# Retention and feed-forward kernel, one core: states summed into other banks, and the order of the batch loop turned

## The reference

```python
xn = layernorm(x)                              # per token over 128 features
q, k, v = xn @ Wq, xn @ Wk, xn @ Wv            # 8 heads of 16
# retention in chunks of 64 tokens, per head:
attn    = (q_c @ k_c.T) * D                    # decayed causal mask
o_intra = attn @ v_c
o_inter = (q_c * decay_q) @ S
S       = decay_s * S + (k_c * decay_k).T @ v_c
att = concat_heads(o_intra + o_inter) @ Wo
h = xn @ w1 + gate * low_rank(xn)              # w1, w2 are ternary with a scale for each row
ffn = (relu(h) ** 2) @ w2
out = x + att + ffn
```

## Time and profile before

| what | value |
|---|---|
| runs | 129.81, 127.7, 129.81 us; median 129.81 |
| the profiled execution | 129.01 us, of which the span of the instructions is 127.0 us |
| PE busy | 117.0 us (92%) |
| DVE busy | 99.2 us (78%) |
| ACT busy | 78.7 us (62%) |
| POOL busy | 64.0 us (50%) |
| TensorE granted clock, mean | 0.997 |
| chain that ended last | PE 80%, DVE 10%, issue 4%, ACT 2%, POOL 1% |

### The profile page before, as it was taken

How to read it: one execution, slowest core, us unless ns; L and a number is a source line. 1 busy time by engine, 2 the same in 40 slices (tenths; PEclk the granted TensorE clock), 3 DMA queues, 4 the chain that set the end, 5 groups by cost and what they waited for, 6 DMA issues and landing times.

```text
span 127.0 us, 6564 instructions
## 1 busy us (share of the span) xinstructions
PE 117.0 (92%) x2860; PEld 92.8 (73%) x2860; DVE 99.2 (78%) x261; ACT 78.7 (62%) x158; POOL 64.0 (50%) x60
## 2 busy tenths in 40 slices
PE   4979999988999999499999999999999999499991
PEld 4425869856688778377788778878897889377890
DVE  0788795489799969858699979896999799729832
ACT  3265669967871897227972897188738774382910
POOL 7099803984439161923439252916193529544400
PEclk9999999999999999999999999999999999999998
DMA  3849920000023000400023001300020002000202
GB/s 105 296 149 320 389 92 34 0 3 5 8 90 81 5 0 23 145 7 0 0 92 74 0 0 53 112 0 0 0 83 0 0 0 83 0 5 0 88 5 83
DMA packets 3357, 7.71 MB, mean 61 GB/s; under 512 B 384, under 2 KB 896, under 8 KB 3216
## 3 DMA queue, kind: packets, MB, share of 16 engines
q1 hardware_dynamic: 2880, 7.01, 16.3%
q10 hardware_dynamic: 464, 0.50, 1.2%
HBM read 5.42 MB, written 2.10 MB: 59 GB/s over the span
## 4 chain that ended last, share of the span: by engine, by line
PE 80%; DVE 10%; issue 4%; ACT 2%; POOL 1%; DVEq 0%; POOLq 0%
PE ps_work L659 10%; PE ps_score L735 8%; PE ps_work L663 7%; PE ps_work L660 7%; PE ps_score L705 6%; PE ps_score L747 5%; PE ps_score L781 5%; PE ps_y L761 4%; PE ps_y L762 4%; PE ps_score L720 3%; DVE sums_of L532 3%; PE ps_turn L668 3%; PE ps_y L765 2%; DVE xn L491 2%; PE ps_turn L692 1%
## 5 line engine op out<-in xcount | busy, mean ns | idle before, releaser
L300 POOL TENSOR_TENSOR sq_lo<-square,sq_hi 128x512 fp32r<-128x512 f32 x31 | 39.8, 1295 | 36.2 <-ACT sq_hi L356 36.2
L347 ACT ACTIVATE square<-ps_work 128x512 f32<-128x512 f32 x32 | 19.1, 596 | 23.1 <-PE ps_work L663 22.6
L516 DVE TENSOR_TENSOR scores<-ps_score,cst 128x512 f32<-128x512 f32 x32 | 20.3, 682 | 1.6 <-PE ps_score L705 1.6
L305 POOL TENSOR_TENSOR q_pair<-q_dec,cst 128x1024 f32<-128x1024 f32 x7 | 13.3, 1894 | 15.9 <-DVE q_dec L501 15.9
L356 ACT ACTIVATE sq_hi<-square 128x512 fp32r<-128x512 f32 x32 | 20.1, 627 | 0.1
L352 ACT ACTIVATE square<-square 128x512 f32<-128x512 f32 x32 | 18.9, 630 | 0.1
L491 DVE TENSOR_SCALAR xn<-x_in,mean_var,rstd 128x128 f32<-128x128 f32 x32 | 14.9, 528 | 0.3
L659 PE MATMUL ps_work<-xn_hi,w_hi 128*128 128x512 f32 x32 | 14.3, 447 | 0.4 <-issue 0.4
L735 PE MATMUL ps_score<-scores,v_pad 64*32 64x64 f32 x1024 | 12.5, 225 | 1.6 <-issue 1.6
L663 PE MATMUL ps_work<-xn_lo,w_hi 128*128 128x512 f32 x32 | 12.6, 394 | 0.0
L660 PE MATMUL ps_work<-xn_hi,w_lo 128*128 128x512 f32 x32 | 12.6, 393 | 0.0
(11 more groups left out here) (123 smaller groups left out, 238.6 us busy)
## 6 DMA issues: line engine op xcount, KB each, us to landing
x_in<-x_tok SPq DMA_DIRECT2D x8, 256.0 KB, 3.4
resid<-x_feat SPq DMA_DIRECT2D x1, 2048.0 KB, 7.7
out_feat<-resid SPq DMA_DIRECT2D x7, 256.0 KB
po_in<-ffn_weights SPq DMA_DIRECT2D x1, 320.0 KB, 3.2
fc_in<-ffn_weights SPq DMA_DIRECT2D x1, 256.0 KB, 3.7
q_table<-q_decay SPq DMA_DIRECT2D x1, 256.0 KB, 3.5
wqvk<-qvk_weights ACTq DMA_DIRECT2D x1, 192.0 KB, 3.9
cst<-const ACTq DMA_DIRECT2D x1, 129.0 KB, 3.9
```

Of the source, the lines that this page charges most:

```text
L300: nc.gpsimd.tensor_tensor(sq_lo[p][:, f, :], square[p][:, f, :], sq_hi[p][:, f, :].bitcast(F32), ALU.subtract).then_inc(lo_ready, 1)
L347: nc.scalar.activation(square[b.parity][:, f, :], ps_work[f % 2][:], ACT.Relu).then_inc(relu_ready, 1)
L516: nc.vector.tensor_tensor(scores[:, g].rearrange("p t s i -> p (t s) i"), ps_score[:, g].rearrange("p (a i) -> p a i", i=BLK), causal.unsq ...
```

## The change

Banks: `ps_turn` and `ps_y` become the two halves of one tensor `ps_both`. Both sides of v and k by token go there in every batch, the first too, and `gather_states` sums into it, no longer into banks 2 and 3 of `ps_score`. The masks run in the order 0 to 3. The first layer's weight is built in bank 3 of `ps_score` and not in `ps_y`.

Order: `gather_states` follows `score` directly. `own_values` and `carry` of batch b stand in front of q, k, v of b+1, in the same body, where `carry` stood in the next one. The turning of `xn` of b+1 waits for all states of b to be read. On VectorE the statistics are taken two batches ahead, `variance` stands behind `decay_q`, `take_states` between the first and the second mask, `add_states` behind `low_xn`, `low_o` of b at the end of b's own body. On ScalarE `root` and `high_o` move with them. On GpSimd `spread_q` stands behind all four `low_square`. In VectorE's and ScalarE's lists the last two of the six bodies are written out (`over_middle`). Products of one column (`place_program`) stand at three places; the warm-up's wide products are fewer.

```diff
+        ps_both = pb("ps_both", [P, ROWS, SEQ])
+        ps_turn, ps_y = ps_both[:, 0, :], ps_both[:, 1, :]
+        w1_bank = ps_score[:, NG - 1, :]
 GpSimd:
             def body(b):
-                for f in range(2):
+                for f in range(NF):
                     low_square(b, f)
                 spread_q(b.step(1))
-                for f in range(2, NF):
-                    low_square(b, f)
 ScalarE:
+            def body(b, more):
                 take_relu(b, 0)
                 take_relu(b, 1)
-                root(b.step(1))
+                take_relu(b, 2)
                 take_square(b, 0)
+                high_square(b, 0)
                 take_square(b, 1)
-                high_square(b, 0)
-                high_o(b.step(-1))
-                take_relu(b, 2)
+                take_relu(b, 3)
+                round_xn(b.step(1))
                 high_square(b, 1)
-                round_xn(b.step(1))
-                take_relu(b, 3)
                 take_square(b, 2)
+                high_square(b, 2)
                 take_square(b, 3)
-                high_square(b, 2)
+                high_square(b, 3)
+                high_o(b)
                 copy_k(b.step(1))
                 copy_k_tok(b.step(1), 0)
-                high_square(b, 3)
                 copy_k_tok(b.step(1), 1)
+                if more:
+                    root(b.step(2))
 VectorE:
+            def body(b, more):
+                before, after, later = b.step(-1), b.step(1), b.step(2)
-                statistics(after)
-                statistics_done(after)
-                take_states(before)
-                variance(after)
-                for k in range(3):
-                    add_states(before, k)
                 for step in range(4):
                     inverse_root(after, step)
                 normalise(after)
-                low_o(before)
+                mask_scores(b, 0)
+                take_states(b)
+                for g in range(1, NG):
+                    mask_scores(b, g)
                 low_xn(after)
-                for g in MASK_ORDER[:2]:
-                    mask_scores(b, g)
+                for k in range(3):
+                    add_states(b, k)
                 finish(before, ps_y)
+                if more:
+                    statistics(later)
+                    statistics_done(later)
                 decay_q(after)
-                for g in MASK_ORDER[2:]:
-                    mask_scores(b, g)
+                if more:
+                    variance(later)
+                low_o(b)
-                for side in range(2):
-                    take_v(after, side)
+                take_v(after, 0)
+                take_v(after, 1)
 TensorE:
             def gather_states(b):
                 pe.wait_ge(zeroed, ZEROED)
-                pe.wait_ge(scores_ready, b.count(NG, ROWS))
+                pe.wait_ge(v_ready, b.count(2, 2))
...
-                            ins = mm(ps_score[g * GW:(g + 1) * GW, ROWS + r, t * GW:(t + 1) * GW],
+                            ins = mm(ps_both[g * GW:(g + 1) * GW, r, t * GW:(t + 1) * GW],
+            def place_program(n, bank, data):
+                for k in range(n):
+                    rows = slice(k % NG * GW, (k % NG + 1) * GW)
+                    mm(bank[rows, 0:1], data[rows, 0:GW], data[rows, 0:1], start=True, stop=True, skip_group_check=True)
...
+            own_values(first)
+            place_program(17, ps_score[:, NG - 1, :], ident)
+            carry(first)
+            def hidden_and_scores(b):
                 pe.wait_ge(q_ready, b.count(1, 1))
                 hidden(b, 0)
                 pe.wait_ge(k_ready, b.count(1, 1))
                 hidden(b, 1)
+                hidden(b, 2)
+                pe.wait_ge(o_lo_ready, b.count(1, 0))
+                score(b)
+                gather_states(b)
+                hidden(b, 3)
+
+            def body(b):
+                before, after = b.step(-1), b.step(1)
+                hidden_and_scores(b)
+                turn_xn(after, b)
                 second_product(before, ps_y, range(NF))
+                pe.wait_ge(relu_ready, b.count(NF, NF))
                 output_product(before, ps_y)
+                own_values(b)
+                carry(b)
-                project_q(after, b)
-                project_k(after, b)
+                project_q(after)
+                project_k(after)
                 project_vk(after, 0)
                 project_vk(after, 1)
-                gather_states(b)
-                own_values(b)
```

More of the change, by code:

```diff
@@ L85, in over_batches, with over_middle @@
         body(Batch(half, 2))
+def over_middle(engine, body):
+    with engine.Fori(0, NB // 2 - 2) as half:
+        body(Batch(half, 1), True)
+        body(Batch(half, 2), True)
+    body(Batch(NB // 2 - 2, 1), True)
+    body(Batch(NB // 2 - 2, 2), False)
 def build(nc, x_tok, x_feat, qvk_weights, ffn_weights, rank_weights, const, q_decay, out_feat):
@@ L395, in _ @@
             take_square(first, 1)
+            high_square(first, 0)
+            take_square(first, 2)
             take_relu(first, 3)
             round_xn(first.step(1))
[L398 removed]
             act.wait_ge(proj_turned, 1)
@@ L598, in _ @@
             nc.vector.tensor_tensor(wo_lo[:], ps_y[:, 0:D], wo_hi[:].bitcast(F32), ALU.subtract).then_inc(y_free, 1)
+            for k in range(3):
+                add_states(first, k)
             take_v(after, 0)
             take_v(after, 1)
+            statistics(first.step(2))
+            statistics_done(first.step(2))
+            variance(first.step(2))
+            low_o(first)
             dve.wait_ge(resid_loaded, 16)
-            def body(b):
-                before, after = b.step(-1), b.step(1)
-                statistics(after)
-                statistics_done(after)
-                take_states(before)
-                variance(after)
-                for k in range(3):
-                    add_states(before, k)
+            def body(b, more):
+                before, after, later = b.step(-1), b.step(1), b.step(2)
                 for step in range(4):
@@ L629, in finish_half @@
                                                op0=ALU.mult, op1=ALU.add).then_inc(y_free, 1)
-            over_batches(dve, body)
+            over_middle(dve, body)
             before = last.step(-1)
-            take_states(before)
-            for k in range(3):
-                add_states(before, k)
-            low_o(before)
-            for g in MASK_ORDER:
+            mask_scores(last, 0)
+            take_states(last)
+            for g in range(1, NG):
                 mask_scores(last, g)
-            finish(before, ps_y)
-            take_states(last)
             for k in range(3):
                 add_states(last, k)
-            dve.wait_ge(hi_ready, last.count(NF, NF))
-            nc.vector.tensor_tensor(sq_lo[last.parity][:, NF - 1, :], square[last.parity][:, NF - 1, :],
-                                    sq_hi[last.parity][:, NF - 1, :].bitcast(F32),
-                                    ALU.subtract).then_inc(last_low_ready, 1)
+            finish(before, ps_y)
             dve.wait_ge(o_done, last.count(1, 1))
@@ L683, in project_vk @@
             def project_vk(b, side):
-                if side == 1 and b is first:
-                    pe.wait_ge(q_ready, b.count(1, 1))
-                elif side == 1:
+                if side == 1 and b is not first:
                     pe.wait_ge(y_free, b.count(1, 0))
@@ L803, in _ @@
             project_vk(first, 1)
-            score(first)
-            after = first.step(1)
-            pe.wait_ge(v_ready, 2)
-            pe.wait_ge(w1_split, 1)
-            for f in range(NF):
-                hidden(first, f)
-            turn_xn(after)
+            after = first.step(1)
+            pe.wait_ge(q_ready, 1)
+            pe.wait_ge(w1_split, 1)
+            hidden(first, 0)
+            pe.wait_ge(k_ready, 1)
+            hidden(first, 1)
+            hidden(first, 2)
+            score(first)
+            gather_states(first)
+            hidden(first, 3)
+            turn_xn(after, first)
             pe.wait_ge(proj_ready, 1)
@@ L816, in _ @@
             ins.then_inc(proj_turned, 1)
-            gather_states(first)
-            own_values(first)
+            project_q(after, first)
             pe.wait_ge(wo_ready, 1)
@@ L821, in _ @@
             nc.tensor.transpose(ps_y[:, 0:D], wo_scaled[:], ident).then_inc(wo_turned, 1)
-            project_q(after, first)
             project_k(after, first)
@@ L862, in _ @@
-            pe.wait_ge(o_lo_ready, before.count(1, 1))
-            score(last)
-            second_product(before, ps_y, range(2, NF))
-            output_product(before, ps_y)
-            hidden(last, 2)
-            for _ in range(6):
-                mm(ps_turn[0:GW, 0:1], ident[0:GW, 0:GW], ident[0:GW, 0:1], start=True, stop=True)
-            gather_states(last)
-            hidden(last, 3)
```

(14 more changed lines are left out.)

97 lines of the change are left out of this document (41 added, 56 removed).

## The result

The changed kernel takes 148.71 us (median of 146.63, 147.87, 149.55 and 150.43), the kernel before 129.6 beside it. Their ratio to the kernel before is 1.146 (95% interval 1.107 to 1.184). Forecast were 139.9 us within 128.5 to 144. The sign and the mechanism of the main term came out, the size did not: the time lies outside the range. The profiled execution took 149.55 us for a span of 147.5.

What follows compares the result with a forecast made beforehand. TensorE's products were taken to bound the kernel, 13.10 us a batch. Batch 1's third sum ending at 39.2, five periods of 15.5 (77.5), 3.93 and 17.3 gave a span of 137.9, so 139.9 us, range 128.5 to 144.

Steps and rivals of the forecast that it cites:

- main term: VectorE's three sums of the states per batch, held by GpSimd's `sq_lo`, keep TensorE waiting 1.8 us at `carry`.
- Sums held by `sq_lo`: In each batch all three sums of the states wait out GpSimd's `low_square` 1 to 3; 1.8 us at `carry`.
- rival 1: First sum slips ahead of `low_square` 1, only two are held: 1.4 less in each of seven batches, 130.0; chance 0.19.
- Rival 2: Sums of the states not held: period 13.7, 127.3 us, or 123.8 with `var_eps` free; chance 0.11 shared with rival 4, written order without effect.
- `var_eps` held by `q_pair`: VectorE's `var_eps`, behind `decay_q`, falls into GpSimd's `spread_q` and lasts until it ends, near 1.8 us.
- `xn` free: VectorE's `normalise` no longer overlaps GpSimd: 1.03 us, regaining the 1.0 it lost before.
- the root behind `var_eps`: On ScalarE `root` waits for `var_eps` and the first relu stands behind it, from A+5.05 to 5.65 (A: third sum's end).
- `hidden` 2 waiting for the first relu: On TensorE `hidden` 2 needs the relu's bank and starts at 5.7 after the third sum; with the turning, 0.8 us waiting.
- TensorE's floor of 12.9: TensorE's own time per batch: two instead of three returns to full products save some 0.2, giving about 12.9 us.
- Start: Until batch 1: first `hidden` at 27.2 instead of 24.89, shorter warm-up costing 0, up to 0.5 if the clock falls back.
- rival 3: More is late: instruction fetch hits again, or the first batch is 1 to 2 later: 142 to 145 us; chance 0.08.
- last stretch: Last batch on TensorE, from body start to the end: 17.3 us where it was 19.16, with sums again held.

Runs made afterwards that it cites:

- fourth experiment: The changed kernel with the earlier kernel's warm-up, GpSimd waiting for the sums, and the variance ahead of the decayed q, all together: 132.07 us.
- second experiment: The changed kernel with GpSimd waiting for the sums of the states before parts 1 to 3 of the squares' rest: 136.27 us.
- ninth experiment: The changed kernel without its 17 and 13 one-column products before the state share and the last own values: 147.23 us.
- third experiment: The changed kernel with the variance of the batch two ahead taken before the decayed q, not behind it: 145.87 us.
- seventh: The kernel before with the changed kernel's short warm-up (40 small products, 1.5 wide ones): 141.3 us.
- eighth experiment: The kernel before with a long warm-up of 40 small products and four and a half wide ones: 136.25 us.
- fifth: The changed kernel with quiet sums, early variance and a long warm-up (40 small products, four and a half wide): 133.88 us.

## Why the prediction was right in its mechanism and wrong in its time

*Sums held by `sq_lo`: right.* Forecast were ends of 3.96, 5.37 and 6.78 behind the start of `take_states`; batch 3 has 4.14, 5.52 and 6.88. The wait at `carry` was 1.8 forecast and is 1.79. Luck had a part: all three sums are held because the first comes behind `low_square` 1, by 0.3 in the forecast and by 0.15 in the trace, so rival 1 was nearer than its chance says. Rival 2 priced the waits at 7 x 1.8 = 12.6; they are 10.9 over all eight batches, since batch 0, 2 and 7 wait less, and taking them away gave 11.0 back.

*`var_eps` held by `q_pair`: right.* It ends 0.03 behind `q_pair`, as forecast, and takes 1.74; without it five periods were 2.6 shorter, for 3.0 (the whole run 1.5). No row had shown this overlap; the nearest row carried it.

*`xn` free, the root behind `var_eps`, `hidden` 2 waiting for the first relu: right*, and with them the period: 15.37 to 15.86 in four of the five full ones for 15.5.

*TensorE's floor of 12.9: wrong by 0.3.* With nothing held it is 13.2 to 13.3 (fourth experiment). The return to full products that is saved is spent: the three `hidden` in a row take 2.44, where nine products at 0.23 are 2.07, mostly since `hidden` 2 waits for the relu of `hidden` 0. It did not enter the sum, as the sums bounded the period, but it would have made rival 2 too fast.

*Start, the step that failed.* The prediction set the shorter warm-up to 0, since it ends before the normalised data is there, or "up to 0.5" if the clock falls back. It cost 3.2: with the longer warm-up the scores of batch 0 begin at 17.36 in place of 20.57. I had looked at when the data is there, not at what TensorE does until then: it is idle for 1.6 us from 6.36 on and then runs at half pace for 9. In the traces with a longer warm-up the clock's record begins, at the full level, at 6.1 to 8.9 us, while products run. With the short one it begins at 17.0 to 18.3, or, in the second and ninth experiment, at about 6, and the level is gone again from 9 to 10 until 16 to 17. Whether the idle time or the shorter work before it brings that about isn't separated.

*Stops of instruction fetch, left out of the sum.* They stood in rival 3 with a chance of 0.08, and even its 142 to 145 is too low. The changed kernel has 1.27 in `carry` of batch 0 and 1.50 in `gather_states` of batch 1. Forecast was `carry` of batch 1 at 39.3, measured 45.4; these 6.1 us are in two steps. The first `hidden` of batch 1 came at 32.47 for 27.2: 3.2 of pace, 1.3 for the stop, and 0.5 at the one-column products, which with the wait behind them take 0.85 (29.22 to 30.07) for 0.3; 0.3 has no answer. The other 0.8 is the stop that ends at 38.00, which kept `take_states` back.

*The rest.* Five periods took 79.3 us for 77.5, of which 1.0 is the one from 76.94 to 93.63, where the granted clock is 0.90. The last stretch took 22.8 for 21.1: again a piece at the lower level (from 126.2 to 129.6, mean of the stretch 0.93), which costs 1.7. The stop of 0.64 in its `own_values` costs nothing, since `carry` still waits 0.52 for the sums behind it. 6.1 + 1.8 + 1.7 = 9.6, which is 147.5 less 137.9. The kernel before shows no such drop until its end, and the two undisturbed runs of the changed one, with granted clocks of 0.999 and 1.000, none or next to none; they are 147.25 and still outside the range. The changed kernel has the same 1.8 us of idleness in most batches and a drop in two of them, the third experiment's trace has the idleness and no drop at all; what brings it on isn't settled.

That the stops are the fetch of instructions is shown twice: their places shift with the length of TensorE's list to the pass (seventh and eighth experiment), and each ends 1.2 to 1.6 us behind the end of a 16 KB packet of instructions (fifth). What sets the moment at which such a packet starts is open.

## What to carry to other kernels

Before moving a step on VectorE, look at what GpSimd does in its new place: here a sum with two SBUF inputs (0.39 free, 1.33 held) and a `tensor_scalar` of 4 columns (0.17 free, 1.74 held) that started under a two-input GpSimd instruction lasted until that one ended, and a chain of dependent small sums pays it once for each link. A single wait on GpSimd, which had time to spare, took 11 us from one kernel and 3.4 from the other, of which only 1.7 are the sums. The warm-up and the number of instructions ahead of a loop are part of a kernel's tuning and have to be priced when they change, by the pace of the first products and by the stops.

## What the runs showed of the hardware that I had not expected

- A two-input sum on VectorE beside one-input GpSimd instructions is hardly held (0.39 median, 0.50 mean), beside two-input ones it is (1.33 mean).
- With the short warm-up TensorE ran at half pace from 8 to 17 us, 512 columns 0.43 apart, not 0.23. The clock column says 1.00 there for want of a record; the second experiment's says 0.50.
- 27 more products ahead of the loop cost the kernel before some 6 us in stops of up to 2.6 us (1.6 in all before), all inside runs of small products.
- Every stop of 0.27 us or more ended 1.2 to 1.6 us behind the end of a 16 KB packet of instructions, and three products more in the list moved four stops by exactly their six passes.
